# Chunk attention: the values' matmuls visited two groups at a time, with a longer ring of exponentials and 16-wide blocks of values

## The reference, cut to what matters

```python
def _L0_attn_a_ref(x, Wq, Wk, Wv):          # x: (16, 512, 128)
    H = 16
    Q = (x @ Wq.T).reshape(H, b, s, dkh)    # dkh = dvh = 8
    K = (x @ Wk.T).reshape(H, b, s, dkh)
    V = (x @ Wv.T).reshape(H, b, s, dvh)
    scores = jnp.einsum('hbqd,hbkd->hbqk', Q, K)
    atten = jax.nn.softmax(scores, axis=-1)
    out = jnp.einsum('hbqk,hbkd->hbqd', atten, V).reshape(b, s, -1)
    y = out + x
    mu = jnp.mean(y, axis=(1, 2), keepdims=True)
    var = jnp.var(y, axis=(1, 2), keepdims=True)
    return (y - mu) / jnp.sqrt(var + EPS)
```

## Time and profile before

| | us |
|---|---|
| three runs, median (lowest to highest) | 3949.91 (3944.6 to 3952.15) |
| the profiled execution, device time | 3944.43 |
| its span in the trace | 3942.7 |
| chunk attention in it, first maximum to last visit | 42.5 to 874.8 |
| one step of chunk attention in the middle | 25.17 |

### The profile page before, as it was taken

One profiled execution on the slowest core, in us unless ns is written; L12 is line 12 of the kernel. 1 busy time (PEld: TensorE's weight loads), 2 busy tenths in 40 slices (PEclk: granted clock), 3 DMA queues, 4 the chain that ended last, 5 costly groups with the idle time before them and its releaser, 6 DMA issues. The chain is left out here.

```text
span 3942.7 us, 89530 instructions
## 1 busy us (share of the span) xinstructions
PE 3455.3 (88%) x30494; PEld 2111.7 (54%) x30494; DVE 2757.4 (70%) x7236; ACT 2286.2 (58%) x5520; POOL 2169.0 (55%) x2263
## 2 busy tenths in 40 slices
PE   5999999985695999999999999995958885987678
PEld 1333333325592566566566566563946774775456
DVE  6888888856454778878888888873437884655565
ACT  2777777763243666666666666662436671864367
POOL 3333333315544777888887888874422332754275
PEclk7999999995697999999999999997979997987879
DMA  5434334413452222222222222222633332110001
GB/s 100 61 59 60 60 60 62 62 17 101 137 193 67 48 55 50 51 56 55 53 57 51 51 57 51 50 55 75 199 92 81 89 82 43 44 45 5 0 1 44
DMA packets 414451, 254.32 MB, mean 65 GB/s; under 512 B 251418, under 2 KB 340434, under 8 KB 412722
## 3 DMA queue, kind: packets, MB, share of 16 engines
q1 hardware_dynamic: 403316, 226.43, 25.0%
q0 software_dynamic: 10688, 22.17, 1.8%
HBM read 91.61 MB, written 45.94 MB: 35 GB/s over the span
## 5 line engine op out<-in xcount | busy, mean ns | idle before, releaser
L2799 POOL TENSOR_TENSOR ra_prob<-ra_prob,ra_inverse 128x256 f32<-128x256 f32 (+3 forms) x512 | 631.1, 1255 | 250.5 <-DVE ra_inverse L3098 249.3
L2577 DVE TENSOR_REDUCE ca_mx<-ca_ps_s 128x2 f32<-128x1024 f32 x512 | 600.6, 1211 | 120.4 <-PE ca_ps_s L2449 120.2
L3012 ACT ACTIVATE ra_prob<-ra_ps_s,ra_low 128x128 f32<-128x128 f32 (+3 forms) x1024 | 533.6, 532 | 228.5 <-DVE ra_low L3078 225.8
L2514 ACT ACTIVATE ca_pT<-ca_ps_p 128x512 f32<-128x512 f32 x1024 | 544.9, 600 | 204.6 <-PE ca_ps_p L2459 203.1
L3078 DVE CUSTOM_DVE_ANT_0 ra_ps_s<-ra_ps_s,ra_mask 128x128 f32<-128x128 f32 (+3 forms) x1024 | 479.9, 510 | 44.1 <-PE ra_ps_s L2954 43.8
L2449 PE MATMUL ca_ps_s<-ca_kst,ca_qst 128*128 128x512 bf16 x1024 | 393.0, 389 | 24.4 <-DMA ca_kst<-ca_bounce 10.9
L2459 PE MATMUL ca_ps_p<-ca_qst,ca_kst 128*128 128x512 bf16 x1024 | 386.7, 383 | 5.5 <-ACT ca_pT L2514 4.2
L3018 ACT COPY ra_probT<-ra_ps_t 128x512 f32<-128x512 f32 x384 | 227.2, 592 | 254.2 <-PE ra_ps_t L2866 254.2
L2866 PE MATMUL ra_ps_t<-ident,ra_prob 128*128 128x128 f32 x2560 | 350.1, 276 | 3.3 <-ACT ra_probT L3018 2.1
L2954 PE MATMUL ra_ps_s<-ra_kz,ra_qz 64*128 64x128 f32 (+3 forms) x2048 | 348.1, 458 | 3.8 <-DMA ra_kz<-ra_rot 2.9
L2792 POOL TENSOR_TENSOR ra_rot<-ra_prod 128x512 f32<-128x512 f32 x256 | 320.6, 1273 | 40.6 <-DVE ra_prod L3087 40.6
(11 more groups left out here) (491 smaller groups left out, 7278.5 us busy)
## 6 DMA issues: line engine op xcount, KB each, us to landing
ra_qz<-ra_rot SPq DMA_DIRECT2D x512, 64.0 KB, 2.0
ra_kz<-ra_rot SPq DMA_DIRECT2D x512, 64.0 KB, 2.0
moe_w_own<-moe_w1T SPq DMA_DIRECT2D x71, 256.0 KB
moe_w_own<-router_w SPq DMA_DIRECT2D x71, 256.0 KB
ca_kst<-ca_bounce SPq DMA_DIRECT2D x256, 64.0 KB
ca_bounce<-ca_thirds SPq DMA_DIRECT2D x192, 64.0 KB
ca_qst<-ca_bounce SPq DMA_DIRECT2D x64, 192.0 KB
moe_hs<-moe_rows SPq DMA_DIRECT2D x71, 66.0 KB, 2.1
```

What stands on the lines that cost most here:

```text
L2514: nc.scalar.activation(pT[:, (NS * hp + u) % PRING, :], ps_p[n % NP][:], ACT.Exp).then_inc(sg["drained"], 1)
L2577: nc.vector.tensor_reduce(mx[:, hm % 2, 2 * j:2 * j + 2], ps_s[m % 2][:].rearrange("p (b k) -> p b k", b=2), AX.X, ALU.max)\
L2799: nc.gpsimd.tensor_tensor(at, at, inverse[:, n % PROB, 2 * tile:2 * tile + 2].unsqueeze(2).broadcast_to([P, 2, keys]), ALU.mult)\
L3012: nc.scalar.activation(prob[:, n % PROB, tile, head, 0:keys], part(n, tile)[:, head, :], ACT.Exp, bias=low[:, n % PROB, at:at + 1], scale= ...
```

## The change

Three edits, all in `chunk_attention`:

- The visits are made in twos. `values(0)` and `values(1)` stand behind unit 11, `values(2)` and `values(3)` behind unit 19, `values(4)` and `values(5)` behind unit 27, `values(6)` and `values(7)` behind unit 3 of the next step. Between two such double visits lie 8 units where 4 lay between single ones.
- The ring `pT` has 16 slots, and ACT's wait for a slot is written to match (`u // 4 - 3` for `u // 4 - 2`).
- The values' blocks are 16 columns wide, one after the other, with a block more at the end of each half. The weights of a values' matmul are still 32 columns: the block's own 16 and the 16 that follow. The first 9 rows of a stripe of `ps_o`, which alone are read, are the same. ACT's blanking of `vst` at the start writes 1584 columns where it wrote 3072.

```diff
-    VRING = 6
-    PRING = 12
+    VRING, VW = 6, 16
+    PRING = 16
...
-        vst = sb("vst", [P, VRING, NC, 4, 32])
+        vst = sb("vst", [P, VRING, NC * 4 + 1, VW])
...
                     for b in range(4):
                         a = 4 * g + b
-                        last = nc.tensor.matmul(ps_o[b * 32:(b + 1) * 32, :], vst[:, h % VRING, a, kt, :], pT[:, (NS * h + 4 * r + b) % PRING, :],
+                        last = nc.tensor.matmul(ps_o[b * 32:(b + 1) * 32, :], vst[:, h % VRING].rearrange("p n d -> p (n d)")[:, (4 * a + kt) * VW:(4 * a + kt) * VW + 32], pT[:, (NS * h + 4 * r + b) % PRING, :],
                                                 start=(kt == 0), stop=(kt == 3))
...
                         if u == 3 and hl is not None:
+                            values(6, hl)
                             values(7, hl)
-                        if hp is not None and u % 4 == 3 and u >= 7:
+                        if hp is not None and u in (11, 19, 27):
+                            values((u - 11) // 4, hp)
                             values((u - 7) // 4, hp)
...
-                            wait(act, sg["pv_done"], 8 * hp + u // 4 - 2)
+                            wait(act, sg["pv_done"], 8 * hp + u // 4 - 3)
```

More of the change, by code:

```diff
@@ L2505, in front_part @@
                             act.wait_ge(sg["pv_done"], 8 * (h - VRING + 1))
-                        nc.scalar.copy(vst[:, h % VRING, :, :, 0:DK], ps_p[n % NP][:, 0:HT].rearrange("p (a k d) -> p a k d", a=NC, k=4)).then_inc(sg["drained"], 1)
+                        nc.scalar.copy(vst[:, h % VRING, 0:NC * 4, 0:DK], ps_p[n % NP][:, 0:HT].rearrange("p (n d) -> p n d", d=DK)).then_inc(sg["drained"], 1)
                 def body(h, ht, hp):
@@ L2522, in _ @@
                 for ring in range(0, VRING, 3):
-                    at = vst[:, ring:ring + 3].rearrange("p r a k d -> p (r a k) d")
-                    blank = core.ones[:, 0:1].unsqueeze(2).broadcast_to([P, 3 * NC * 4, 32])
+                    at = vst[:, ring:ring + 3].rearrange("p r n d -> p (r n) d")
+                    blank = core.ones[:, 0:1].unsqueeze(2).broadcast_to([P, 3 * (NC * 4 + 1), VW])
                     nc.scalar.activation(at, blank, ACT.Copy, scale=0.0).then_inc(v_set, 1)
@@ L2527, in _ @@
                 for ring in range(0, VRING, 3):
-                    at = vst[:, ring:ring + 3, :, :, DK].rearrange("p r a k -> p (r a k)")
-                    nc.scalar.copy(at, core.ones[:, 0:1].broadcast_to([P, 3 * NC * 4])).then_inc(v_set, 1)
+                    at = vst[:, ring:ring + 3, :, DK].rearrange("p r n -> p (r n)")
+                    nc.scalar.copy(at, core.ones[:, 0:1].broadcast_to([P, 3 * (NC * 4 + 1)])).then_inc(v_set, 1)
                 static_steps(NHALF, (FRONT, TURN, PROB), body)
```

## The result

Slower, as forecast: a median of 3979.4 us (six runs, 3972.1 to 3986.7) against 3948.3 (six runs, 3939.4 to 3952.2). The ratio is 1.0081, with a 95% interval of 1.0064 to 1.0098. The profiled execution took 3981.1, with a span of 3979.4.

A forecast was written before the change was run, and what follows sets the result against it. PE was taken to bound the stage, DVE as runner-up. The terms summed to 33.4, taken as +33 us on the profiled 3944.4, making 3977.4; with the runs' median 5.5 above the profiled one, 3983, range 3968 to 4002.

The forecast's parts named there:

- The walk: Between double visits PE waits 0.40 us for the third pair's bank, 0.27 for the fourth's; eight units take 6.14 (before 5.66).
- The second visit: In a double visit on PE, the second visit runs on as a second pass does and adds 0.91 us.
- The bound below: The least that a double visit's second visit could add on PE: 0.91 us at best, with 1.09 at worst.
- last sign: The prediction is wrong if the visits' second half on PE costs other than 0.91 us.
- The no-overlap rival: The two visits of a pair don't overlap: the second costs 1.09 us, +23 on top, 4006 in all; 13%.
- DVE's other work: Transposition and reciprocal, 0.83 us between two reductions, cost nothing, standing where DVE idles ahead of a stretch's first pair.
- The sum: Whole stage: 27 steps +27.0 us, halves 28 and 29 +3.4, halves 30 and 31 +3.5, half 0 -0.5; 33.4.
- The ring, the blocks, the blanking: Longer ring and blocks of 16 cost no time; shorter blanking of `vst` at the start: nothing, at best 2 us off.
- even case: Rival: PE's waits are a quarter of the walk's, so gain and loss meet at 3950 us; 4%.
- the faster one: Rival: PE doesn't wait for the third pair's bank, which needs reductions under 0.82 us; 22 less, 3928; 5%.
- The clock: Rival: PE's added waits lower the granted clock; a tenth over one 100 us would be 10 us more; 3%.

The follow-up runs named there:

- e4: The changed kernel with the single visits of before, so only the ring of 16 and blocks of 16 remain: 3940.2 us against 3940.8 before, ratio 0.9997.
- e1: The kernel before with DVE's maxima taken over the first 256 of each score's 512 columns: 3924.9 us against 3940.8 before, ratio 0.9951.
- e2: The changed kernel with DVE's maxima taken over the first 256 of each score's 512 columns: 3919.7 us against 3940.8 before, ratio 0.9945.
- e7: Ring and blocks of 16, PE's list of a step rewritten, one double visit (groups 5 and 6), against the kernel before: 3919.6 us against 3941.7, ratio 0.9940.
- e8: The same rewritten list as e7, but groups 5 and 6 visited apart, so all visits single: 3921.1 us against 3941.7 for the kernel before, ratio 0.9949.

## Why the prediction was right, point by point

The prediction was 3983 in a range of 3968 to 4002, and it came out at 3979.4. The mechanism was right, and the closeness of the number is in part luck: the walk's sum was 33.4 for the stage, which grew by 27.8, and the medians differ by 31.2, some 3 more than the stage in the two traces, with nothing changed behind it. The step is 26.00, just below the 26.1 to 26.2 that the prediction named.

- **The walk.** The third pair's score was to start 0.62 after the matmul before, the fourth's 0.48: 0.62 and 0.47, with 0.37 where the transposition stands, also as said. DVE was to be free for 1.5 before a stretch's first pair: 1.48, in good part filled with the transposition or the statistics. The stretches were 6.14, 6.14, 6.36 and 7.54, and are 6.10, 6.10, 6.31 and 7.49.
- **The second visit.** This is the term that was off: 0.91 was taken, and it is 0.86 (1.86 for both, less 1.00). The pass that I took as the measure, a visit's second one, is itself 0.02 longer than the ones that follow it. All four stretches are 0.04 to 0.05 shorter for that, 5 to 6 us over the stage. The bound below, 0.91 "at best", was no bound, and by the prediction's own last sign ("if the visits' second half costs other than 0.91") this term failed, if only by 0.05. The no-overlap rival, 13%, falls with the rows of the loads.
- **DVE's other work.** It was put at nothing. The stretch of units 4 to 11 has the transposition and reciprocal ahead of it, the next one the statistics, and both are 6.10: nothing it is.
- **The sum.** In the trace the last visit starts at 902.6 where it was 874.8, so the stage grew by 27.8, not 33.4. The parts: the 27 steps 22.1 (27.0 was said), the steps of halves 28 and 29 2.8 (3.4), those of 30 and 31 4.0 (3.5), all before that -1.1 (-0.5). The first is the second visit's 0.05 four times a step.
- **The ring, the blocks, the blanking.** Nothing, by e4.
- **The even case and the faster one.** The even one needed waits of a quarter of the walk's, and they were as walked; the faster one needed reductions of under 0.82. e1 and e2 made them 0.69, and there the double visits do win, by 0.49 a step.
- **The clock.** A granted clock of 1.00 in both stretches shown, as before, with the waits in them.

What isn't settled is the rest of the program. The medians differ by 31 us, the two profiled executions by 36.7, and the stage in these by 27.8. From the last visit to the end of the span it is 3068 in the one of before, 3077 in the one of after, and 3063 to 3069 in the nine experiments, where nothing behind the stage was changed. e2 is the changed kernel but for the length of its reductions, and has 3065. So the 9 us more are most likely this one execution's and not the change's. Some 6 of them arise in the next layer, within 175 us of the last visit: ACT there waits for PE 26.41 before a copy in the kernel before (the copy starts at 1041.90) and 31.16 after (1076.22). Why is open.

## What to carry to other kernels

Before grouping work on the bounding engine to save its switches, count how many pieces of the other engines' work then fall into one stretch, and compare that with the buffers between them: two pairs of banks cover two pairs, and the third waits (here 0.40 us, the fourth 0.25). Here grouping paid where the engine had something else to do between the pieces, and it cost where it hadn't, for one and the same edit. A step in which PE's row is busy for 25.08 of 25.17 us still hid 1.0 us that another order of the same work gave back, about half of it waits and half joins of matmuls of one width.

## What the runs showed of the hardware that was not expected

- Visits of 32-column weights joined end to end run on without a gap: the third and fourth pass begin 0.43 after the one before, the second 0.45. The way in and out (0.09 and some 0.1) is paid once. It is shared in the same way by a visit and the projection of 32 columns behind it in e7 (0.11 and 0.09), and fp32 projections of 128 columns right behind a visit took 0.96 in e8, against 0.87.
- In a run of reductions the next starts 0.08 before the row of the last ends: four of 1.21 take 4.62, and not 4.84. A walk must take the pitch, 1.14, for how fast they follow one another, and the end of the row for when the bank comes free.
